# One attention and feed-forward kernel: the order of the step loop, the drain and the second half on four engines

## What is computed

```python
q = (hidden_states @ w_q).reshape(B, S, H, Dh)
k = (hidden_states @ w_k).reshape(B, S, H, Dh)
v = (hidden_states @ w_v).reshape(B, S, H, Dh)
mask = dilated_mask(S)   # same segment of 64, or distance a multiple of 4 up to 256
scores = jnp.einsum('bqhd,bkhd->bhqk', q, k) * scaling + mask[None, None]
attn = jax.nn.softmax(scores.astype(jnp.float32), axis=-1).astype(q.dtype)
out = jnp.einsum('bhqk,bkhd->bqhd', attn, v).reshape(B, S, H * Dh)
return out @ w_o
```

## Time and profile before

| | |
|---|---|
| median of three runs | 467.28 us (466.55 to 468.51) |
| span of the profiled execution | 468.2 us |
| TensorE busy | 443.3 us, 95% of the span |
| VectorE busy | 394.1 us, 84% |
| ScalarE busy | 333.0 us, 71% |
| GpSimd busy | 296.5 us, 63% |

### The profile page before, as it was taken

How to read it: one execution, slowest core, us unless ns; L and a number is a source line. 1 busy time by engine, 2 the same in 40 slices (tenths; PEclk the granted TensorE clock), 3 DMA queues, 4 the chain that set the end, 5 groups by cost and what they waited for, 6 DMA issues and landing times.

```text
span 468.2 us, 17264 instructions
## 1 busy us (share of the span) xinstructions
PE 443.3 (95%) x6440; PEld 348.8 (74%) x6440; DVE 394.1 (84%) x1344; ACT 333.0 (71%) x975; POOL 296.5 (63%) x491
## 2 busy tenths in 40 slices
PE   7999699999999999999999899998987989999996
PEld 5687588888888888888787678887744757558775
DVE  5888598997988899799797697996899989998775
ACT  3678668778768777877786678695566579987533
POOL 4222576687576768667865587665669897674322
PEclk9999999999999999999999999999999999999999
DMA  6477952356345335445455564464000000000003
GB/s 224 175 254 201 276 122 53 75 115 123 75 84 110 74 74 109 81 78 109 86 116 122 110 135 90 77 123 91 1 1 0 0 2 0 2 0 2 1 0 91
DMA packets 136098, 40.53 MB, mean 87 GB/s; under 512 B 104976, under 2 KB 131024, under 8 KB 136016
## 3 DMA queue, kind: packets, MB, share of 16 engines
q1 hardware_dynamic: 135440, 38.38, 35.9%
q10 hardware_dynamic: 576, 1.05, 0.6%
HBM read 29.44 MB, written 9.96 MB: 84 GB/s over the span
## 4 chain that ended last, share of the span: by engine, by line
PE 59%; POOL 9%; DMA 8%; DVE 8%; ACT 7%; SPq 4%; issue 3%; ACTq 0%; POOLq 0%; DVEq 0%
PE psum L464 10%; PE psum L422 10%; PE psum L484 5%; PE psum L1186 5%; PE psum L498 5%; PE psum L495 4%; PE psum L510 4%; PE psum L403 4%; DMA st<-w_rows_dram 3%; DMA w_rows_dram<-st 3%; PE psum L1181 3%; ACT pband L569 3%; PE psum L405 2%; PE psum L404 2%; POOL area L1827 2%
## 5 line engine op out<-in xcount | busy, mean ns | idle before, releaser
L948 POOL TENSOR_SCALAR pband<-pband,fac 128x192 f32<-128x192 f32 x256 | 103.9, 424 | 84.8 <-DVE fac L771 84.7
L569 ACT ACTIVATE pband<-pband,st 128x192 f32<-128x192 f32 x256 | 113.2, 448 | 0.9 <-DVE st L719 0.9
L719 DVE CUSTOM_DVE_ANT_0 pband<-psum,band_mask 128x192 f32<-128x192 f32 x256 | 76.0, 353 | 0.1
L422 PE MATMUL psum<-keys,q_class 64*64 64x192 f32 (+2 forms) x1536 | 66.3, 274 | 0.0
L464 PEld LDWEIGHTS psum<-ident,pband 128*128 128x128 f32 x384 | 45.3, 141 | 25.5 <-issue 17.8
L464 PE MATMUL psum<-ident,pband 128*128 128x128 f32 x384 | 53.1, 273 | 6.1 <-DVE arena L836 3.1
L422 PEld LDWEIGHTS psum<-keys,q_class 64*64 64x64 f32 x1536 | 57.7, 133 | 1.4 <-issue 1.4
L569 ACT ACTIVATION_READ_ACCUMULATOR pband<-pband,st 128x1 f32 x256 | 49.5, 193 | 0.0
L938 POOL COPY q_class<-q_rows 128x512 f32<-128x512 f32 x32 | 36.4, 1137 | 14.0 <-ACT q_rows L609 14.0
L930 POOL COPY keys<-k_rows 128x512 f32<-128x512 f32 x32 | 36.2, 1131 | 14.3 <-issue 7.2
L780 DVE COPY pt<-psum 128x512 f32<-128x512 f32 x64 | 43.6, 682 | 0.4
(11 more groups left out here) (213 smaller groups left out, 1086.4 us busy)
## 6 DMA issues: line engine op xcount, KB each, us to landing
v_rows_dram<-arena SPq DMA_DIRECT2D x32, 256.0 KB, 4.6
v_both<-v_rows_dram SPq DMA_DIRECT2D x32, 256.0 KB, 3.9
v_seg<-v_rows_dram SPq DMA_DIRECT2D x64, 128.0 KB, 3.8
v_side<-v_rows_dram SPq DMA_DIRECT2D x96, 64.0 KB, 2.6
w_rows_dram<-st SPq DMA_DIRECT2D x64, 8.0 KB, 3.0
st<-w_rows_dram SPq DMA_DIRECT2D x64, 8.0 KB, 2.5
arena<-_attn_hidden_states_dram SPq DMA_DIRECT2D x4, 256.0 KB, 3.9
out_dram<-x SPq DMA_DIRECT2D x4, 256.0 KB, 2.5
```

Of the source, the lines that this page charges most:

```text
L422: return pe.matmul(bank[2 * r + head][rows, at:at + y.shape[1]], x, y, start=True, stop=True, skip_group_check=True)
L569: act.activation(x, x, ACT.Exp, bias=mine[:, head:head + 1], scale=-1.0, accum_out=mine[:, 2 + head:3 + head]).then_inc(s_exp, 1)
L719: dve.tensor_tensor_reduce(pband[:, G % P_SLOTS, c, head, :], bank[2 * r + head][:, at:at + BAND], band_mask[:, (0, 1, 1, 2)[w], SEG * (1 ...
L948: pool.tensor_scalar(x, x, fac[:, F % 2, 1, c, head:head + 1], 1.0, ALU.mult, ALU.mult).then_inc(s_scaled, 1)
```

## The change

No instruction is added or taken away; all four computing engines get other lists. SyncE's list stays.

- **Loop, TensorE.** In one round of the loop the old order is T0, W2, S0, W3, S1; the new one is S0, W2, S1, W3, T0. The rest of the round (PQ, T1, T2, PK, W0, W1, T3, O) keeps its order. The loop now begins in the middle of the group, so the indices read one higher.
- **Loop, VectorE.** The old round is D, E0, F, BM0, SM0, E2, SM1, BM1, SS, ACC; the new one is BM0, ACC, SM0, D, E0, F, SM1, E2, BM1, SS. D and F of a step thus stand behind BM0 and SM0 of the round. `quantise` goes from between E0 and F to the end; `split_qk` from behind E0 to between D and E0.
- **Loop, ScalarE.** B0 keeps its place behind the first score half; B1 goes behind `take_keys` and `seg_exps`; X goes behind the B0 of the next step and TO.
- **Loop, GpSimd.** `scale_seg` goes ahead of the keys, and queries are sorted in the round of their keys.
- **Run-in.** S1(3), T0(0), PQ(5), T1(0) and T2(0) are in the first round of the loop now, in this order. On VectorE, D(1), BM0(3) and SM0(3) stand behind the last `take_values`, and SS(2) behind it too; on ScalarE B1(2) stands behind the last `take_values`.
- **Drain and second half.** New lists on four engines; the largest move is that E0(29) stands ahead of D(30), and D(31) behind the first pieces of the next sublayer (`x1`, `bn0`, `ag0`, `qx0`).

```diff
@@ block.tensor, the loop
             for t in range(FIRST_STEP, DRAIN):
+                weigh(t - 7, 2)
+                scores(t - 3, 1)
+                weigh(t - 7, 3)
+                turn(t - 6, 0)
+                project(t - 1, 0)
+                turn(t - 6, 1)
+                turn(t - 6, 2)
                 project(t, 1)
                 weigh(t - 6, 0)
                 weigh(t - 6, 1)
                 turn(t - 6, 3)
                 output(t - 7)
-                turn(t - 5, 0)
-                weigh(t - 6, 2)
                 scores(t - 2, 0)
-                weigh(t - 6, 3)
-                scores(t - 2, 1)
-                project(t, 0)
-                turn(t - 5, 1)
-                turn(t - 5, 2)
@@ block.scalar, the loop
             for t in range(FIRST_STEP, DRAIN):
-                exp_difference(t - 4)
-                take_out(t - 6)
-                take_queries(t)
-                odd_turned(t - 5, 1)
-                take_keys(t + 1)
-                band_exps(t - 2, 0)
-                odd_turned(t - 5, 3)
-                seg_exps(t - 2)
-                band_exps(t - 2, 1)
+                band_exps(t - 4, 1)
+                odd_turned(t - 7, 3)
+                band_exps(t - 3, 0)
+                take_out(t - 7)
+                exp_difference(t - 5)
                 if t in (6, 7):
                     split_qk(1, 7 - t)
+                take_queries(t - 1)
+                odd_turned(t - 6, 1)
                 if t in (QUANT_STEP + 2, QUANT_STEP + 7, QUANT_STEP + 12):
                     coarse_weights((t - QUANT_STEP) // 5)
+                take_keys(t)
+                seg_exps(t - 3)
@@ block.vector, end of the run-in and the loop
-            take_values(19); seg_sums(1); seg_max(2, 0); seg_max(2, 1); band_max(2, 0); take_values(21); seg_sums(2)
-            take_values(23); band_max(2, 1); differences(0); take_values(25); factors(0); seg_max(3, 0)
-            take_values(27); band_max(3, 0); take_values(29); differences(1); take_values(31); even_turned(0, 0)
-            factors(1); even_turned(0, 2); seg_max(3, 1); seg_sums(3); band_max(3, 1)
+            take_values(19); seg_sums(1); seg_max(2, 0); seg_max(2, 1); band_max(2, 0); take_values(21)
+            take_values(23); band_max(2, 1); differences(0); take_values(25); factors(0); take_values(27)
+            take_values(29); take_values(31); seg_sums(2)
             for t in range(FIRST_STEP, DRAIN):
-                differences(t - 4)
-                even_turned(t - 5, 0)
-
+                band_max(t - 3, 0)
+                accumulate(t - 8)
+                seg_max(t - 3, 0)
+                differences(t - 5)
                 if t in (7, 8):
                     split_qk(1, 8 - t)
...
-                factors(t - 4)
-                band_max(t - 2, 0)
-                seg_max(t - 2, 0)
-                even_turned(t - 5, 2)
-                seg_max(t - 2, 1)
-                band_max(t - 2, 1)
-                seg_sums(t - 2)
-                accumulate(t - 6)
@@ block.gpsimd, the loop
             for t in range(FIRST_STEP, DRAIN):
-                scale_band(t - 5, 1)
-                keys_by_class(t)
-                scale_seg(t - 5)
-                scale_band(t - 4, 0)
-                queries_by_class(t - 1)
+                scale_band(t - 8, 1)
+                scale_seg(t - 8)
+                keys_by_class(t - 3)
+                scale_band(t - 7, 0)
```

More of the change, by code:

```diff
@@ L554, in _ @@
[L554 to L558 removed]
+            weigh(26, 2); weigh(26, 3); turn(27, 0); turn(27, 1); scores(30, 1); scores(31, 0); weigh(27, 0)
@@ L836, in take_values, with zero_pads @@
                 dve.tensor_copy(v_slot(i), turn_bank[i % 2][:, :]).then_inc(s_vev[i % 2], 1)
+            def zero_pads():
+                dve.wait_ge(s_wlo, 4)
+                dve.memset(raw[P - R:P, 0:2, 2 * P:FT], 0.0)
+                dve.memset(raw[:, 2, FF:FT], 0.0).then_inc(s_zero, 1)
             def blocks(x):
```

179 lines of the change are left out of this document (93 added, 86 removed), and 16 rows, old and new, of the table STEPS.

## The result

The changed kernel is slower: 474.15 us median of six runs (471.85 to 476.6) against 468.38 of the kernel before beside it, ratio 1.0109 with a 95% interval of 1.0072 to 1.0146. Forecast were 465.4 us and a range of 462.3 to 469.3. The profiled execution has a span of 473.5 us, 5.3 more than before. TensorE's busy time hardly tells: 448.1 us against 443.3, 95% of the span both times.

A forecast was written before the change was run, and what follows sets the result against it. TensorE's own work was taken to bound the loop. Terms 0 (loop), -1.9 (late statistics), +0.8 (run-in), -1.0 + 0.2 (drain), 0 (second half) sum to -1.9 us: span 468.2 to 466.3, time 465.4 us; range 462.3 to 469.3.

The forecast's parts named there:

- The second half, 0 from -1 to +1: Last output of attention to the end: neighbours trade places, the chain passes on the earlier start; 0 us, -1 to +1.
- own sign of being wrong: Would be wrong: a late-loop D wait that still stops TensorE, or a second half differing by over 1 us.
- 0.14 for slower: Chance of a time above 469.6 us, made of most of rival (b) and a little of another rival.
- rival (b): Loop: E0 becomes the bound, T2 starts 0.3 us late each round; 472.9 us, or 469.2 if only short rounds; chance 0.14.
- The quantisation "lies in idle time": End of VectorE's loop round: work of 7.4 us of 8.80 leaves idle time for the quantisation, costed at nothing.
- The run-in, +0.8, bounds -0.4 to +1.5: Before the loop: T1(0)'s stall mostly goes, but send(2) leaves about 1.6 us later, delaying D(3) and T2(2); +0.8 us.
- The loop, 0: TensorE's loop rounds: same work reordered, entry and exit of small shapes unchanged; 0 us, from +1.5 to -2.8.
- Rival (a): Loop: TensorE's round gets 0.11 us shorter, entry from O hidden; -2.8 us over 25 rounds, 462.6 us; chance 0.18.
- Late statistics, -1.9: Late loop: D comes later in the round, so its 3.83 us wait shrinks to about 0.4; -1.9 us, 0 to -2.6.
- The drain, -0.8: Drain: E0(29) ahead of D(30) frees T2(29) from 1.39 us idle, -1.0; more shape changes, +0.2.
- From the span to the time: Whole kernel: median of runs taken 0.9 us below the profiled span, so span 466.3 gives 465.4 us.

The follow-up runs named there:

- experiment 6: Experiment 1 plus one exchange of the new second half, on VectorE qx7(1) ahead of ag0(2); ratio 1.0049 to the kernel before, second half 128.51 us.
- experiment 11: Experiment 8 with the whole new second half of the changed kernel; ratio 1.0041 to the kernel before, second half 128.52 us.
- experiment 7: Changed kernel with two second-half exchanges taken back (GpSimd qa1(1) ahead of qb4(0), VectorE ag0(2) ahead of qx7(1)); ratio 1.0025 to the kernel before.
- experiment 12: Experiment 8 with two second-half exchanges: ScalarE xqt(2) ahead of qa6(0), GpSimd qb4(0) ahead of qa1(1); ratio 0.9992 to the kernel before.
- experiment 1: Changed kernel with all four engines' lists from output 31 on as in the kernel before; 469.14 us, ratio 0.9968 to the kernel before.
- experiment 10: Experiment 8 with D ahead of BM0 again in VectorE's round from t = 9 on; 467.16 us, ratio 0.9975 to the kernel before.
- experiment 9: Experiment 8 with both exchanges: GpSimd qb4(0) ahead of qa1(1), VectorE qx7(1) ahead of ag0(2); ratio 0.9976 to the kernel before.
- experiment 5: Experiment 1 plus one exchange of the new second half, on GpSimd qb4(0) ahead of qa1(1); ratio 0.9981 to the kernel before.
- experiment 3: Changed kernel with the quantisation moved from the end of VectorE's round to behind E0 in the next round; 474.16 us, ratio 1.0084 to the kernel before.
- experiment 2: Kernel before with only the changed kernel's lists from output 31 on; 473.32 us, ratio 1.0071 to the kernel before.
- experiment 4: Changed kernel with SS(2) and B1(2) back ahead of the last copies of values and split_qk behind E0; 471.52 us, ratio 1.0017 to the kernel before.
- experiment 8: Experiment 1 with experiment 4's run-in mends and the quantisation's first piece behind E0 of the next round; 466.54 us, ratio 0.9944 to the kernel before.

## Why the prediction was wrong

- **The second half, 0 from -1 to +1: this is the step that failed**, by 5.2 us. "Neighbours trade places" and a chain that passes on a shift was an argument about the whole where each exchange had to be read. 0.62 us is one VectorE instruction ahead of an aggregate that heads a chain over GpSimd to TensorE (experiment 6). 0.3 us is a longer wait before t2(2) (experiment 11; 1.65 in experiment 7 too, so neither of the two exchanges taken back there makes it). 1.2 us is a race between qa7(0) and qb4(0) that two exchanges turn round together (experiment 12). The rest, 0.2 to 0.3, lies behind it. 2.8 us is the clock, for which the sum had no term. The prediction's own sign of being wrong, a second half that differs by over 1 us, came; its 0.14 for slower stood on rival (b), which did not happen.
- **The clock.** No step of the prediction asked where TensorE would stand long enough for its clock to fall. In the profiled execution it fell behind the new wait of 2.12 us (run-in) and inside that of 2.78 (second half); it did not fall at 2.21 in experiment 1, at 2.77 in experiments 11 and 12, or at the 3.06 of before. Falls are more frequent where waits are longer: with 1.62 us before t2(1) 8 of 12 executions were at the upper level, with 2.24 us and the same other lists 2 of 12 (experiments 1 and 6, two sessions); within one session 11 of 12 with 1.61 (experiment 10) and 4 of 12 with 2.24 (experiment 9). That the longer wait itself lets the clock fall is argued, not shown: in experiment 9 the profiled fall came 70 us later, behind 0.74 us.
- **The quantisation "lies in idle time": wrong**, by 1.7 us in the round of output 6. VectorE's idle time was there, but GpSimd was at work in it, and the small instruction stood when the weights came late (four of six profiled executions); before, the piece stood where GpSimd is idle. Rival (b) looked for E0 as the bound with copies that take the same time in every round; they do, no copy out of PSUM stood in the rows read.
- **The run-in, +0.8, bounds -0.4 to +1.5.** The mechanism was named, one step too late: D(2) and T2(1) at 67 us, not D(3) and T2(2) near 75. T2(0) came at 56.85, better than the 58.2 forecast, and send(2) went out 0.9 later, not 1.6. Where the clock did not fall, output 1 came 0.74, 1.1 and 1.4 later than in the profile of before (experiments 1, 5 and 3); with its fall 2.29. But the run-in of before has falls too: against such an execution (80.99, experiment 2) the changed kernel's output 1 is only 0.12 later. The term was right in kind; the range lacked the clock, on both sides.
- **The loop, 0**: right. -0.6 us in 18 rounds; O pays the entry, T0 saves it. Rival (a) is out, and so is (b): rounds of 9.23 and 8.76, no T2 waiting for E0 in the middle of the loop. But (b) was nearer than it looked. From the end of S0 to PQ the sum had 3.1 us in a short round and 3.5 in a long one; the trace has 2.81 and 3.28, against 3.00 for VectorE's work up to D. In the short rounds E0 starts straight behind D, 0.42 us after PQ instead of 0.28, and still ends in time.
- **Late statistics, -1.9**: right in cause (experiment 10) and, between the two profiled executions, in size, -2.04; the late rounds of before scatter by 1.6 us from one execution to another (experiment 2), so that the size has some luck in it. D's wait stayed at 1.41 where 0.4 was forecast, so one round is still 10.25.
- **The drain, -0.8**: right in sign, -1.19. T2(29) no longer waits.
- **From the span to the time.** I took the span 0.9 us above the median of the runs and carried that over. But a time here is 1.8 to 2.1 us above its span (475.48 for 473.5), so the profiled execution of before was one of about 470.2 us, and the kernel before has medians between 468.4 and 471.0 in its later runs. Span has to be compared with span: the forecast span of 466.3 is a time of about 468.3, not 465.4.

## What to carry to other kernels

When a change reorders lists, go through the exchanges one at a time: for each instruction that moves back, who waits for it and how long that engine already waits there. Before counting an idle stretch on VectorE as a free place for work over SBUF, look at what GpSimd does in it; a race of the two within some tenths of a microsecond is a price of its own, which other exchanges can turn round. Where a change makes TensorE stand longer, add a second term beside the wait, the work behind it at half speed in some of the executions, and look at the mean clocks of many executions: one profile can be of either kind.

## What the hardware showed that I had not expected

- Some instructions on VectorE stand until GpSimd's is done, and the other way round. The one that begins first goes on: 0.95 and 2.03 us when VectorE was 0.16 ahead, 2.02 and 1.39 when GpSimd was 0.12 ahead. The Trainium skill (SBUF — State Buffer, "Who interferes with whom") states that a VectorE instruction with two inputs in SBUF contends with a GpSimd instruction that reads SBUF, and that the order of issue decides who blocks; the trace agrees with the numbers above.
- The one that stands may lose more than once: the 24-column instruction of experiment 4 let the rest of one GpSimd group and two further instructions pass and ended with the last of them, 2.52 us for 0.18. Early in a row of four short GpSimd pieces it gets in between (0.41 to 0.49 us). The reduction just ahead of it (L855, 0.55 us) lost nothing to the same GpSimd row: 0.54 where GpSimd is idle (experiment 3).
- TensorE's granted clock fell to its lower level for 3 to 7 us at a time, inside or up to 1.4 us behind waits of 0.74 to 3.38 us, in some executions and not in others of the same kernel. Over the twelve executions of experiments 1 and 2, 0.01 less of mean clock goes with 4.3 us more of span in either (2.6 to 5.6 in the other kernels). That is part of the scatter, and it can be tuned: in experiment 8 no execution had such a fall, and the spans still ranged from 463.6 to 466.9 us.
- What stays open: which moved piece makes the 0.3 us before t2(2), and why the clock falls at a wait in one execution and not in the next.
